# The next x turned between the variance and the q feature, and its cast ahead of k's exponentials

## The reference

```python
h = _layernorm(x, axis=-1) * (1 + ca) + sa
q = _feature_map(h @ Wq.T + bq)      # elu(z) + 1
k = _feature_map(h @ Wk.T + bk)
KV = einsum('bhsd,bhsm->bhmd', k, v) # over all 8192 rows
Z = 1.0 / (einsum('bhsd,bhd->bhs', q, k.sum(axis=2)) + 1e-06)
x = x + ga * (attn(q, KV, Z) @ Wo.T + bo)
```

## Time and profile before

| | us |
|---|---|
| median of 3 runs | 1182.32 (1181.68 to 1182.43) |
| profiled execution | 1182.51 |
| its span, first to last instruction | 1180.8 |
| TensorE busy | 1163.4 |
| VectorE busy | 980.5 |
| GpSimd busy | 601.9 |
| ScalarE busy | 539.2 |

### The profile page before, as it was taken

One profiled execution on the slowest core, in us unless ns is written; L12 is line 12 of the kernel. 1 busy time (PEld: TensorE's weight loads), 2 busy tenths in 40 slices (PEclk: granted clock), 3 DMA queues, 4 the chain that ended last, 5 costly groups with the idle time before them and its releaser, 6 DMA issues.

```text
span 1180.8 us, 18181 instructions
## 1 busy us (share of the span) xinstructions
PE 1163.4 (99%) x5456; PEld 969.5 (82%) x5456; DVE 980.5 (83%) x2242; ACT 539.2 (46%) x1095; POOL 601.9 (51%) x458
## 2 busy tenths in 40 slices
PE   8999999999999999999999999999999999999998
PEld 5888888788887788888788888888888888888886
DVE  6998788988889988887788888888888888888875
ACT  4555445455544545555353434434435344354441
POOL 1434443433343443443565666667666666676632
PEclk9999999999999999999999999999999999999999
DMA  6565544543443434444413453444544544445321
GB/s 231 167 194 179 168 138 135 160 135 107 124 128 107 141 110 132 121 141 125 108 46 114 148 164 129 145 153 127 165 137 141 162 132 144 145 138 164 112 86 54
DMA packets 168834, 161.01 MB, mean 136 GB/s; under 512 B 16712, under 2 KB 115440, under 8 KB 168736
## 3 DMA queue, kind: packets, MB, share of 16 engines
q1 hardware_dynamic: 168736, 159.85, 43.7%
HBM read 95.30 MB, written 64.49 MB: 135 GB/s over the span
## 4 chain that ended last, share of the span: by engine, by line
PE 80%; DVE 8%; ACT 4%; issue 4%; POOL 2%; DMA 1%; SPq 0%; DVEq 0%; POOLq 0%; ACTq 0%
PE ps L1727 25%; PE ps L1728 25%; PE ps L1734 25%; PE ps L1948 1%; PE ps L1940 1%; POOL cn L758 1%; DVE zk L1381 1%; ACT exp_k L903 1%; DMA wm_in<-in_L_wmod_dram 1%; DVE qf L1357 1%; PE ps L1835 1%; ACT exp_q L874 1%; ACT exp_q L876 1%; DVE zk L1393 1%; ACT exp_k L905 1%
## 5 line engine op out<-in xcount | busy, mean ns | idle before, releaser
L730 POOL TENSOR_TENSOR xn_lo<-xn,xn_hi 128x512 fp32r<-128x512 f32 x64 | 86.1, 1345 | 275.0 <-ACT xn_hi L865 275.0
L746 POOL TENSOR_TENSOR qks<-q_in,ks_q 128x1024 f32<-128x1024 f32 x32 | 77.0, 2407 | 103.0 <-DVE ws L1566 85.6
L758 POOL TENSOR_TENSOR cn<-c,half 128x16 f32<-128x16 f32 x32 | 93.7, 2927 | 37.7 <-DVE c L1484 37.7
L927 ACT CAST xT_hi<-ps 128x512 fp32r<-128x512 f32 x64 | 37.0, 578 | 153.4 <-DVE ps L1457 145.6
L1727 PE MATMUL ps<-wk_hi,xT_hi 128*128 128x512 f32 x256 | 100.8, 394 | 4.7 <-ACT xT_hi L859 4.7
L874 ACT ACTIVATE exp_q<-qf 128x512 f32<-128x512 f32 x64 | 40.5, 633 | 142.1 <-DVE qf L1357 142.0
L1727 PE MATMUL ps<-k_hi,xn_hi 128*128 128x512 f32 x256 | 101.7, 397 | 0.0
L1727 PE MATMUL ps<-wq_hi,xT_hi 128*128 128x512 f32 x256 | 101.1, 395 | 0.1
L1727 PE MATMUL ps<-g_hi,qT_hi 128*128 128x512 f32 x256 | 100.3, 392 | 0.1
L1727 PE MATMUL ps<-v_hi,xT_hi 128*128 128x512 f32 x256 | 100.0, 391 | 0.0
L1728 PE MATMUL ps<-wk_lo,xT_hi 128*128 128x512 f32 x256 | 99.7, 390 | 0.0
(11 more groups left out here) (251 smaller groups left out, 3239.3 us busy)
## 6 DMA issues: line engine op xcount, KB each, us to landing
xin<-_attn_hidden_states_dram SPq DMA_DIRECT2D x64, 256.0 KB, 3.2
q_scratch<-qf SPq DMA_DIRECT2D x64, 256.0 KB, 3.3
xin<-_attn_hidden_states_dram SPq DMA_DIRECT2D x32, 512.0 KB, 4.5
q_in<-q_scratch SPq DMA_DIRECT2D x128, 128.0 KB, 3.0
out_dram<-qf SPq DMA_DIRECT2D x64, 256.0 KB, 2.2
xn_scratch<-xn SPq DMA_DIRECT2D x62, 256.0 KB, 2.0
xq<-xn_scratch SPq DMA_DIRECT2D x248, 64.0 KB, 2.5
x_scratch<-xn SPq DMA_DIRECT2D x56, 256.0 KB, 2.3
```

Source lines behind the costliest of these rows:

```text
L730: nc.gpsimd.tensor_tensor(moved(xn_lo[:, 1 - s, :], i + 1), kept(xn[:, 1 - s, :], i + 1), moved(f32(xn_hi[:, 1 - s, :]), i + 1), ALU.subtr ...
L746: nc.gpsimd.tensor_tensor(qks[:].rearrange("p h (g f) -> p (h g) f", f=P), q_of(j).rearrange("p (n f) -> p n f", f=P), ks_q[:].unsqueeze(1 ...
L758: nc.gpsimd.tensor_tensor(cn[:].rearrange("p h e -> p (h e)"), c2[:].rearrange("p h e -> p (h e)"), half[:], ALU.pow).then_inc(cn_done, 1)
L927: nc.scalar.copy(xT_hi[:, h, :], bank_x2T).then_inc(x2Th_done, 1)
```

## The change

Two orders are changed, one on VectorE and one on ScalarE; no instruction is added or dropped.

- VectorE: from step 1 on, `turned_x` of tile i + 1 comes directly behind the variance (`var_eps`) of tile i + 2, ahead of the modulation and of the q feature. It came behind xn. `xT_low` of tile i + 1 takes the place where `turned_x` was, ahead of the k feature. It came behind it.
- ScalarE: from step 1 on, `xT_high` of tile i + 1 comes ahead of k's exponential instructions. It came behind them.

```diff
@@ ScalarE, step
                 if live(i - 1, T) and i < T - 1:
                     q_exponential(i - 1, 1 - s)
+                if live(i + 1, T) and i > 0:
+                    xT_high(i, s)
                 prepare(i, 0)
                 if live(i, T):
                     act.wait_ge(zk_done, i + 1)
...
                     nc.scalar.activation(exp_k[:, s, :], exp_k[:, s, :], ACT.Exp, scale=-1.0).then_inc(ek_done, 1)
-                    if live(i + 1, T) and i > 0:
-                        xT_high(i, s)
                     act.wait_ge(kf_done, i + 1)
@@ VectorE, step
                     var_eps(i + 2, s)
+                if live(i + 1, T) and i > 0:
+                    turned_x(i + 1, 1 - s)
                 if 1 <= i <= 4 * KB:
                     modulation((i - 1) // KB, (i - 1) % KB)
...
                 if ahead:
                     normed(i + 2, s)
                 if live(i + 1, T) and not early_turn:
-                    turned_x(i + 1, 1 - s)
+                    xT_low(i + 1, 1 - s)
                 if live(i, T):
                     dve.wait_ge(ek_done, i + 1)
...
                     scaled(i)
-                    if live(i + 1, T) and not early_turn:
-                        xT_low(i + 1, 1 - s)
                     dve.wait_ge(kf_done, i + 1)
```

## The result

The changed kernel takes 1225.58 us (median of 4 runs, 1223.42 to 1228.0) against 1182.25 us: a ratio of 1.037, 95% interval 1.035 to 1.039, so 43.3 us slower. It was forecast at 1216.5, in a range of 1200 to 1231. The profiled execution took 1226.17 us, with a span of 1224.5.

The account below looks back on a forecast made before the run. TensorE was taken to bound the kernel, busy 1163.4 of 1180.8 us. Its idle of 15 + 26 = 41 us against 8 before gave +33, plus 2 at the end, +35; +34 was taken: 1216.5 us, range 1200 to 1231.

Parts of the forecast that it names:

- The bound and the prize: First half: TensorE bounds the kernel; its waits for `xT_hi`, 8.0 us together, are all there is to win.
- The trip: xn's way out to DRAM and back as `xq`: 6.3 us from xn's start, so the transpose waits about 1.2 us.
- The circle: xn, store, loads, transpose, q feature, k bias, next xn: 8.18 us per light step against TensorE's 8.16.
- Steps 1 to 16: Steps with a modulation between transpose and q feature: 8.85 us each, about 15 us of TensorE idle in all.
- The slow trips: In steps 1 to 16, SyncE's extra loads slow the round trip: 5.5 us together, bounds 0 and 8.5.
- Steps 17 to 61: Rest of the sweep, where preparation lengthens VectorE's steps: 26 us of TensorE idle in all.
- The `catT` steps: Four steps with 2.75 us of work behind `k_lo`: 9.7 against 8.16 us, 1.55 each, 6.2 together.
- Steps 25 to 37: Forecast for steps 25 to 36: four TensorE products of 2.2 us pay for VectorE's part, leaving 2 us.
- The end of the sweep: From the last k products to q's return, the chain runs over VectorE: 1 to 3 us more, 2 taken.
- That x is there in time: Rival: the regrouped x arrives before its transpose, gaining at most 8.0 us, 1174 to 1182; chance 0.04.
- The quiet landing: Rival: the last `xq` load lands in 1.95 us, light steps make good 0.4, 1199 to 1206 us; chance 0.17.
- The rival that TensorE loses its clock: Rival: idle gaps slow TensorE's clock; ten steps with products taking twice 0.227 us would be 80 us; chance 0.02.

Follow-up runs that it names:

- the run with 13 steps: Changed kernel with cast, transpose and `xT_lo` in their new places in 13 chosen steps only, the old order in all others: 1183.90 us.
- the run without the trip: Changed kernel with `xq` loaded from x itself, ahead of xn's store, instead of from the stored xn: 1183.09 us.
- modulation ahead: Changed kernel with the modulation of steps 1 to 16 placed before the transpose instead of after it: 1218.03 us.
- q's store last: Changed kernel with q's store behind the four loads of `xq` on SyncE's queue instead of ahead of them: 1213.75 us.
- extra issue, changed: Changed kernel with one small spare load on SyncE ahead of the four loads of `xq`: 1234.25 us.
- behind the q feature: Changed kernel with the transpose moved to after the q feature and the modulation: 1211.68 us.

## Why the prediction was right, point by point

**The bound and the prize.** TensorE bounds the kernel before and there was 8 us to win at most. Nothing contradicts it, and none of the 8 us was got: not in the run with 13 steps, and not in the run without the trip, in which no transpose waited and TensorE no longer waited for `xT_hi` (1183.09 us).

**The trip.** Put at 6.3 us from xn to the transpose, 6.1 measured in step 40. The term that was off is the landing behind q's store: 3.52 from the first load to the transpose, not 3.75. The circle was put at 8.18 and is 7.8 to 8.3, 8.05 in the mean of ten light steps, so light steps made good 0.1 us where none was expected. The wait per step was put at 1.2 us: 57.6 us in 40 steps is 1.44.

**Steps 1 to 16.** Forecast 15 us, 11.3 measured. Eleven of the sixteen steps with a modulation took 8.5 to 9.0 us from transpose to transpose (8.85 forecast), the one with sb 9.3 and four 10.0 to 10.5. The slow trips were too dear in the sum: with its other terms as they stand, 2.0 of their 5.5 us are left.

**Steps 17 to 61.** Forecast 26 us, but as TensorE's whole idle, of which about 6 stood there before. 29.0 measured as added time. The `catT` steps with what surrounds them: 7.1 measured for about 7 net. Steps 25 to 37: 7.2 measured for 2. This is the step of the sum that failed: the step with u0, at 251 us, was 16.54 us long where it was 10.56, which is 6.0 of the 7.2. I had only priced VectorE's amount of work, and not that TensorE itself waits for a piece of preparation. It did so for 2.82 us, and then ran slow (below). Steps 38 to 61: 14.6 measured for about 11 net; 3.5 us of it are in step 39, behind b2's rows, and 2.8 in step 51, in which TensorE waited 2.7 and 2.6 us for the q bias. Slow trips came back here that the forecast had left to the first steps: waits for `xq` of over 2 us in steps 50 and 60, and in 33 before them, as in 7, 11, 17 and 24. In step 11 SyncE's issue of x's load held the queue (120.61 below, 0.43 us long in nearly all other steps).

```profile
120.23 0.34 SPq L627 DMA_DIRECT2D xn_scratch<-xn  x1
120.61 1.86 SPq L630 DMA_DIRECT2D xin<-_attn_hidden_states_dram  x1
122.52 0.43 SPq L609 DMA_DIRECT2D q_scratch<-qf  x1
```

In the other six, issues and xn's store were as ever, and the loads themselves landed late: the last one after 3.4 to 4.0 us, where it took 2.7 in step 40. The four loads of step 60, then those of step 40:

```profile
DMA to landing us min/median/max: 2.6/2.8/3.8
...
DMA to landing us min/median/max: 2.2/2.4/2.7
```

What made them late is open.

**The end of the sweep.** 2 us forecast, 2.6 measured, in the k product of the last tile and the sum of k.

**The subtraction.** The 8 us of idle of the kernel before were taken off the sum, though its own table gave 5. With 5, the point would have been 1219.5.

**What was luck.** The mechanism and the circle held. That the sum came within 9 us of the time owes something to misses that ran against each other: some 4 us too dear ahead of step 17, 9 too cheap behind it, a part of these from the slow clock, which the sum had at nothing.

**The rivals.** That x is there in time fell with the 40 waits. The quiet landing was real, but it needed q's store out of the way: 1213.75 us in the run that did that, where the forecast had 1199 to 1206. The rest of that difference is preparation and slow trips, by the account above; no run parts them. The fixed part of 2.0 us with the data on top stands in the Trainium skill (DMA: Bandwidth & Descriptors, Anatomy of one DMA) for transfers that GpSimd issues. The estimate from it for the store is 2.6 us; these stores are SyncE's, and took 2.04 here too. The rival that TensorE loses its clock came true in two steps, at a small part of the price named for it. Its premise was wrong, too: the first half of the kernel before stood at 1.00 throughout, but the trace had a stretch at the slow clock in the second half (below).

## What to carry to other kernels

Before an instruction is moved ahead of another on an in-order engine, ask whether what it waits for is made, by way of other engines and transfers, by something that will now stand behind it: then steps are chained by the whole trip, and slack that let the engine catch up is gone, even when each wait looks small. Sum the circle from the rows (here about 8.05 us) and compare it with the step of the bounding engine (8.16) and with how fast the delayed engine must be able to go (7.0), not with the first alone. A wait that shows no idle in the profile says nothing on how much slack it has; the issue times and landings do.

## What the runs showed of the hardware

TensorE lost its clock in two steps of the sweep. In the changed kernel, the stretches of the u0 step and of step 39 (length, busy times, granted clock, as the earlier trace rows), each with the products behind its wait:

```profile
251.29:267.83 16.54, 13.72 (x46) 10.05 (x46) 11.60 (x20) 7.48 (x13) 4.93 (x5) 0.79 0.42 128
...
257.11 4.71 PE L1835 MATMUL ps<-catT,raw_fv 128*128 128x328 f32 x8 [2.82 <-DVE acc_fv L1149]
...
384.81:397.48 12.67, 9.93 (x38) 7.75 (x37) 11.31 (x20) 4.25 (x7) 3.59 (x3) 0.87 0.25 75
...
393.15 0.80 PE L1727 MATMUL ps<-wq_hi,xT_hi 128*128 128x512 f32 x1 [2.74 <-DVE qf L1357]
393.74 0.63 PE L1728 MATMUL ps<-wq_lo,xT_hi 128*128 128x512 f32 x1
394.17 0.63 PE L1727 MATMUL ps<-wq_hi,xT_hi 128*128 128x512 f32 x1
```

The means of 0.79 and 0.87 are mixes of the two levels, 1.2 and 2.4 GHz: behind an idle time of 2.82 us the eight products took 4.71 us, and behind 2.74 us those of 512 columns started 0.43 us apart in place of 0.227. In the run with only the transpose moved the same products followed 1.54 us of idle and the clock stayed at 1.00:

```profile
250.57:262.86 12.29, 10.75 (x45) 8.31 (x45) 11.12 (x19) 6.34 (x11) 5.12 (x4) 1.00 0.44 137
...
255.13 2.45 PE L1835 MATMUL ps<-catT,raw_fv 128*128 128x328 f32 x8 [1.54 <-DVE acc_fv L1149]
```

In the u0 step of the other slow kernels the products took 4.11 us behind 2.73 us of idle (modulation ahead) and 4.13 behind 2.85 (q's store last), but 2.45 behind 2.68 (extra issue, changed) and 2.44 behind 2.25 (behind the q feature). Step 39 is as mixed: slow behind 3.19 us (extra issue, changed), 2.74 (modulation ahead) and 1.92 (behind the q feature), at full clock behind 2.37 (only the transpose moved). In step 51 the changed kernel kept its clock behind 2.60 us. So the length of the idle time alone does not tell which wait costs the clock.

Of the 4.25 us between the two u0 steps above, 1.3 are idle time and some 3 the slow clock, so one such event costs up to about 3 us, not the 8 that a whole step at half the clock would. In step 39 it cost little: 12.67 us with it, and 12.60 with only the transpose moved, at full clock. The clock is a small part of the loss in all: the execution with only the transpose moved that was profiled stood at 1.00 throughout, and took 1220.29 us, 37.8 more than the kernel before.

That waits inside a loop can send the array back to the slow clock is what the Trainium skill states (TensorE: Matmul & The Clock Gate, HAM oscillation). Here it happened at the two longest waits of the sweep, and not at the 28 waits of up to 1.4 us for `k_lo`. The kernel before, too, has such a stretch, in its second half, behind waits of 0.97 and 0.79 us; the changed kernel has it at the same place, so it is no part of the difference:

```profile
655.50:657.30 1.80, 1.80 (x7) 1.71 (x7) 1.48 (x4) 1.44 (x4) 1.72 (x3) 0.50 0.00 0
```

The second surprise is how much a load of 64 KB minds the 256 KB ahead of it on the queue: 2.6 us in the median behind q's store, 2.0 ahead of it, and 2.3 when a spare issue came between them.
